# Half of a mixing stage moved into a recurrence, and statistics over two heads at once, in a hand-ordered delta-rule and expert kernel

## The reference

```python
q = short_conv(x @ Wq.T); k = short_conv(x @ Wk.T); v = short_conv(x @ Wv.T)
beta  = sigmoid(x @ Wb.T)
delta = delta_rule(l2norm(q), l2norm(k), v * beta, beta)
short = fir(v, 3 taps per channel); longp = fir(v, 63 taps per channel)
paths = (short, longp, delta, v)
stats = [mean and variance of each path over the 64 of each head]
probs = softmax(gate_mlp(concat(x, stats)) / temp)
probs = maximum(probs, floor); probs /= sum(probs)
out = sum(probs[i] * paths[i])
out = out * rsqrt(mean(out ** 2) + 1e-5) * onorm_w
x1 = layernorm(x + out @ Wo.T)
y  = sum over the top 2 of 8 experts of w * down(silu(gate(x1)) * up(x1))
return layernorm(x1 + y)
```

## Time and profile before

| | |
|---|---|
| median of three runs | 1904.76 us |
| lowest and highest | 1901.11, 1905.17 us |
| the profiled execution's own time | 1897.1 us |
| its span | 1895.4 us |
| mean granted TensorE clock | 0.899 |
| PE busy | 1501.2 us (79%), 12507 instructions |
| PE weight loads (PEld) | 1111.5 us (59%) |
| DVE busy | 1353.1 us (71%), 3875 instructions |
| ACT busy | 949.5 us (50%), 1998 instructions |
| POOL busy | 436.7 us (23%) |
| costliest DVE group: taps of phase B (L1465) | 143.4 us, 192 x 747 ns |

### The profile page before, as it was taken

One profiled execution on the slowest core, in us unless ns is written; L12 is line 12 of the kernel. 1 busy time (PEld: TensorE's weight loads), 2 busy tenths in 40 slices (PEclk: granted clock), 3 DMA queues, 4 the chain that ended last, 5 costly groups with the idle time before them and its releaser, 6 DMA issues. The chain is left out here.

```text
span 1895.4 us, 40891 instructions
## 1 busy us (share of the span) xinstructions
PE 1501.2 (79%) x12507; PEld 1111.5 (59%) x12508; DVE 1353.1 (71%) x3875; ACT 949.5 (50%) x1998; POOL 436.7 (23%) x473
## 2 busy tenths in 40 slices
PE   6776065979999999999999999997436999999800
PEld 3446034737747657657567477476225888888700
DVE  6996055687798887887887887976455455554488
ACT  6772161356455654654655564542443555555434
POOL 6783200000030040040120310300233333333300
PEclk9997586989999999999999999987657999999955
DMA  5548632023243243333342333332524533333295
GB/s 198 191 161 256 168 72 72 3 58 100 73 119 99 60 124 102 79 90 101 93 117 81 93 100 87 93 101 63 190 99 134 188 105 103 101 105 100 79 384 192
DMA packets 297373, 224.36 MB, mean 118 GB/s; under 512 B 173472, under 2 KB 265632, under 8 KB 296960
## 3 DMA queue, kind: packets, MB, share of 16 engines
q1 hardware_dynamic: 225600, 158.84, 28.9%
q0 software_dynamic: 15232, 43.53, 6.3%
q10 hardware_dynamic: 56384, 19.93, 4.1%
HBM read 130.42 MB, written 91.82 MB: 117 GB/s over the span
## 5 line engine op out<-in xcount | busy, mean ns | idle before, releaser
L2041 POOL DMA_INDIRECT y_d<-C_yb,C_dest x136 | 131.6, 968 | 235.0 <-ACT C_yb L2152 232.6
L1465 DVE SCALAR_TENSOR_TENSOR B_conv<-B_ps_x,B_cw,B_conv 128x511 f32<-128x511 f32 (+2 forms) x192 | 143.4, 747 | 51.9 <-ACT B_conv L1177 46.9
L422 POOL DMA_INDIRECT xs_d<-x,slot_u x128 | 133.3, 1042 | 136.7 <-DVE m_acc L1867 100.0
L688 POOL MEMSET B_z<- 128x256 f32 (+4 forms) x40 | 5.6, 199 | 690.7 <-DMA B_z<-scr_a 690.7
L1177 ACT ACTIVATE B_conv<-B_ps_x,B_cw 128x512 f32<-128x512 f32 x64 | 43.7, 683 | 167.2 <-PE B_ps_x L745 165.9
L2271 DVE TENSOR_TENSOR C_av<-C_sg,C_ps_g 128x256 f32<-128x256 f32 x136 | 57.2, 421 | 95.2 <-ACT C_sg L2146 95.2
L745 PE MATMUL B_ps_x<-B_xa,B_wk 128*128 128x512 f32 x128 | 68.1, 660 | 65.8 <-DVE B_sel L1457 45.0
L2075 PE MATMUL C_ps_g<-C_w_high,C_xt_high 128*128 x272 | 120.0, 441 | 0.3 <-DVE C_xt_low L2277 0.3
L2283 DVE TENSOR_TENSOR C_avt_low<-C_ps_a,C_avt_high 128x256 fp32r<-128x256 f32 x136 | 57.6, 424 | 85.2 <-ACT C_avt_high L2141 85.2
L2075 PE MATMUL C_ps_g<-C_w_high,C_xt_low 128*128 x272 | 108.3, 398 | 0.0
L2075 PE MATMUL C_ps_g<-C_w_low,C_xt_high 128*128 x272 | 107.4, 395 | 0.0
(11 more groups left out here) (334 smaller groups left out, 4274.4 us busy)
## 6 DMA issues: line engine op xcount, KB each, us to landing
C_xb<-xs_d SPq DMA_DIRECT2D x136, 132.0 KB, 2.1
C_w_high<-y_d SPq DMA_DIRECT2D x12, 1024.0 KB, 14.0
A_band<-fir_long POOLq DMA_DIRECT2D x32, 256.0 KB, 5.6
A_work<-xT SPq DMA_DIRECT2D x16, 512.0 KB, 4.9
v_d<-A_v_tok SPq DMA_DIRECT2D x16, 512.0 KB, 3.5
short_d<-A_sh_tok SPq DMA_DIRECT2D x16, 512.0 KB, 3.2
B_xa<-xT SPq DMA_DIRECT2D x8, 1024.0 KB, 5.6
B_v_tok<-v_d SPq DMA_DIRECT2D x8, 1024.0 KB, 5.4
```

What stands on the lines that cost most here:

```text
L422: pool.indirect_dma_start(t["xs_d"][:, :], bass.IndirectOffsetOnAxis(ap=slot_u[:, c:c + 1], axis=0), x1[:, b, j, :], None).then_inc(done, 16)
L1465: V.scalar_tensor_tensor(conv[:, g % 2, k:], X[g % 2][:, :SEQ - k], cw[:, g // 4, gg % CH, 3 - k:4 - k], conv[:, g % 2, k:], ALU.mult, ALU ...
L2041: pool.indirect_dma_start(t["y_d"][:, :], bass.IndirectOffsetOnAxis(ap=dest[:, q:q + 1], axis=0), yb[:, u], None).then_inc(y_out[u], 16)
```

## The change

All of it is in phase B.

- **Statistics over two heads.** A `bn_stats` now takes 128 numbers, two heads interleaved (stride 64), so that its even positions are one head and its odd ones the other. There are half as many, and the tile `bn` is half as large. `stats` no longer joins even and odd: five operations in place of nine.
- **Second half batch's mixing.** In merging, DVE still does the softmax, weighs the first half batch's `lo` and `delta` and both half batches' `sh`, and finishes the first half batch. The second half batch's weighing of `lo` and `delta`, its sums, its sum of squares and its scaling (`weigh_long`, `add_delta`, `add_rest`, `sum_squares`, `scale_mix` with b = 1) go to the start of the next step's recurrence. So do its squares and root on ACT (`square_mix`, `rms_root`); its squares go to `hid` in place of `sq`.
- **First key taps.** `taps_of(i + 2, 0)` in merging becomes `taps_of(i + 1, 0)` at the start of recurrence.
- **Output by halves.** PE transposes and projects the first half batch's mix as before, and the second one's in turn 1 of the recurrence, behind `solve_rows` and `within`.
- **Order on DVE in the recurrence and `late_rows`.** Output adds, row statistics and path statistics are placed anew; more statistics are left to `late_rows`.
- **Evictions in one row.** PE makes the four groups of products one after the other, ahead of the router and a projection; DVE and ACT evict the four in a row, and `late_rows` follows DVE's last.
- **Path rows by halves.** SP waits for the transposes of one half batch before it loads that half's rows, where it waited for both.
- **Loop.** DVE's loop is now steps 1 to 6.

```diff
-bnst = sb("bn", [P, PT, PATHS, HEADS, 6]); dm = sb("dm", [P, PT, STATS // 2]); gst = sb("gst", [P, PT, 3, STATS])
+bnst = sb("bn", [P, PT, PATHS, HEADS, 3]); gst = sb("gst", [P, PT, 3, STATS])
...
-squares = sq[:].rearrange("p c (a b) -> p (c a) b", b=D)
+squares = [x.rearrange("p c (a b) -> p (c a) b", b=D) for x in (sq[:], hid[:, 0:2])]
...
-            hold(sp, o_turned, 4 * i)
             for b in range(2):
+                hold(sp, o_turned, 4 * (i - 1) + 2 * (b + 1))
...
-            for jj in range(2):
+            for jj in range(4):
+                if jj > 1:
+                    for k in a_kept:
+                        pe.wait_ge(k, 4 * p + jj - 1)
                 a_products(p, jj)
             if last is not None:
                 router(last)
             project(p, 6)
-            for jj in range(2, 4):
-                for k in a_kept:
-                    pe.wait_ge(k, 4 * p + jj - 1)
-                a_products(p, jj)
             pe.wait_ge(beta_ok, 2 * (p + 1))
...
-                project_out(i - 1, 1)
...
+                if has_prev and s == 1:
+                    turn_mix(i - 1, 1)
...
+                if has_prev and s == 1:
+                    project_out(i - 1, 1)
...
+                if b:
+                    pe.wait_ge(ln, LN * i + m + 1)
...
-            pe.wait_ge(o_kept, 4 * (i + 1))
+            pe.wait_ge(o_kept, 4 * i + 2 * (b + 1))
             for jp in range(2):
-                if b:
-                    pe.wait_ge(ln, LN * i + jp + 1)
...
-                turn_mix(i - 1)
+                turn_mix(i - 1, 0)
...
-                keep_o(i - 1)
+                keep_o(i - 1, 0)
             if has_next:
                 group_b(i + 1, 0)
+            if has_prev:
+                square_mix(i - 1, 1)
+            if has_next:
                 group_a(i + 1, 1)
+            if has_prev:
+                rms_root(i - 1, 1)
             for s in range(1, TPB):
+                if s == 1:
+                    keep_u(i, s)
+                    if has_prev:
+                        keep_o(i - 1, 1)
                 if has_next:
                     group_b(i + 1, s)
                     group_a(i + 1, s + 1)
                 if has_prev and s == 3:
                     keep_x1(i - 1, 0)
-                keep_u(i, s)
+                if s > 1:
+                    keep_u(i, s)
                 if has_prev and s == 2:
...
+            weigh_values(i, 0)
+            if has_next:
+                merge(i + 1, 0)
+            weigh_values(i, 1)
+            if has_next:
+                merge(i + 1, 1)
             if has_after:
                 group_a(i + 2, 0)
+            if has_next:
+                merge(i + 1, 2)
+            square_mix(i, 0)
+            rms_root(i, 0)
             if has_next:
                 merge(i + 1, 3)
                 merge(i + 1, 4)
...
-            for jj in range(2):
+            for jj in range(4):
                 keep_even(jj)
             if not first:
                 late_rows(p - 1)
-            for jj in range(2, 4):
-                keep_even(jj)
...
+                for m in range(CH):
+                    out = bnst[:, n_, (0, 1, 3, 2)[k], 2 * m:2 * m + 2, :].rearrange("p h s -> p (h s)")
+                    w = V.bn_stats(out, src[:, m * P:(m + 1) * P].rearrange("p (h d) -> p d h", h=2))
...
+            if has_next:
+                taps_of(i + 1, 0)
+            if has_prev:
+                weigh_long(i - 1, 1)
+                add_delta(i - 1, 1)
             state(0)
+            if has_prev:
+                add_rest(i - 1, 1)
+            bn(0, 2)
+            bn(1, 2)
             output(0)
             if has_prev:
+                sum_squares(i - 1, 1)
             residual(1)
             if has_prev:
+                scale_mix(i - 1, 1)
+                add_out(i - 1, 0)
+            if has_next:
+                taps_of(i + 1, 1)
             state(1)
+            dve.wait_ge(r_out, 4 * i + 1)
+            bn(0, 3)
             output(1)
             if has_prev:
+                row_stats(i - 1, 0)
+
+            residual(2)
+            if has_next:
+                taps_of(i + 1, 2)
+            if has_prev:
                 add_out(i - 1, 1)
                 row_stats(i - 1, 1)
+            bn(2, 2)
+            bn(3, 2)
+            state(2)
+            output(2)
             if has_next:
                 taps_of(i + 1, 3)
             if has_prev:
                 scale_norm(i - 1)
 
             residual(3)
             dve.wait_ge(r_out, 4 * i + 2)
             bn(1, 3)
+            dve.wait_ge(sl_in[0], 16 * (1 + 2 * HEADS) * (i + 1))
+            for q in range(TPB):
+                bn(q, 0, (0,))
+                if q == 1 and has_next:
+                    taps_of(i + 1, 4)
+            bn(0, 1, (0,))
+            bn(1, 1, (0,))
             output(3)
             if not has_next:
                 late_rows(i)
 
         def late_rows(i):
+            bn(2, 1, (0,))
+            bn(3, 1, (0,))
+            dve.wait_ge(sl_in[1], 16 * (1 + 2 * HEADS) * (i + 1))
+            for q in range(TPB):
+                bn(q, 0, (1,))
+                bn(q, 1, (1,))
+            dve.wait_ge(r_out, 4 * i + 3)
+            bn(2, 3)
             dve.wait_ge(r_out, 4 * i + 4)
             bn(3, 3).then_inc(st_dve, 1)
 
...
+            part = lambda k: gst[:, :, k].rearrange("p t (a s) -> p t a s", s=2)
+            high, low = part(0), part(1)
...
+            V.tensor_copy(high[:, :, :, 0].bitcast(F32R), f[:, :, :, 1]).then_inc(st_dve, 1)
+            V.tensor_scalar(high[:, :, :, 1].bitcast(F32R), f[:, :, :, 2], 1.0 / DH, None,
+                            ALU.mult).then_inc(st_dve, 1)
+            dve.wait_ge(st_dve, c + 3)
+            V.tensor_tensor(low[:, :, :, 0], f[:, :, :, 1], high[:, :, :, 0], ALU.subtract).then_inc(st_dve, 1)
+            V.scalar_tensor_tensor(low[:, :, :, 1], f[:, :, :, 2], 1.0 / DH, high[:, :, :, 1], ALU.mult,
+                                   ALU.subtract).then_inc(st_dve, 1)
...
+        def merge_and_mix(i, has_next):
             softmax(i)
+            weigh_long(i, 0)
+            for b in range(2):
+                weigh_short(i, b)
             if has_next:
                 merge(i + 1, 0)
+            add_delta(i, 0)
+            add_value(i, 0)
+            if has_next:
+                merge(i + 1, 1)
             add_rest(i, 0)
             if has_next:
                 merge(i + 1, 2)
+            add_value(i, 1)
             sum_squares(i, 0)
             if has_next:
                 merge(i + 1, 3)
             scale_mix(i, 0)
             if has_next:
                 first_rows(i + 1)
                 merge(i + 1, 4)
...
-        taps_of(1, 0)
...
-        with dve.Fori(1, PAIRS - 2) as i:
+            merge_and_mix(i, has_next)
+        step(0, False, True)
+        with dve.Fori(1, PAIRS - 1) as i:
+            step(i, True, True)
+        step(PAIRS - 1, True, False)
+        weigh_long(end, 1)
+        add_delta(end, 1)
+        add_rest(end, 1)
+        sum_squares(end, 1)
+        scale_mix(end, 1)
```

152 lines of the change are left out of this document (43 added, 109 removed).

## The result

The changed kernel takes 1935.78 us (median of four runs, 1934.89 to 1949.33), the kernel before 1902.93 (four runs, 1898.98 to 1905.17): ratio 1.0197, interval [1.0165, 1.0229]. (The ratio is not the quotient of the two medians, which is 1.0173; by its interval the change costs 31 to 44 us.) By the medians it is slower, as forecast, but by 33 us where 13 were predicted, and 3.8 us beyond the upper end of the range.

The account below looks back on a forecast made before the run. No engine was taken to bound the kernel throughout; when DVE reaches `scale_norm` decides the A stage's start. Recurrence +8.0, A stage +11.4, clock +1.8, ends -8.0 make +13.2 us: 1918.0 from the median 1904.76, range 1898 to 1932.

Parts of the forecast that it names:

- upper end: High end of the range, 1932 us: half clock every step, later edge count (1.5), tail's gain lost (3.6).
- The back edge: DVE's loop branch, merging to recurrence: idle of 1.79 us carried over, now before work others wait for; DVE resumes at 863.8 or 864.4.
- its two counts: Branch idle counted from the last operation's end (DVE resumes 863.8, scale_norm +1.35 us) or its start (864.4, +1.9).
- the rival in which the edge hides: DVE fetches while waiting for the last merge: 1.8 x 5 us goes, total +2.4, 1907 us; chance 0.16.
- The clock: PE idle before x1_ok in recurrence brings half clock: 0 to 1.6 us per step, 0.3 taken, +1.8 in all.
- a rare rival: PE's clock falls in every step: 1.6 us instead of 0.3, six times, +21, 1926 us; chance 0.08.
- The A stage: Four evictions in a row, then a longer late_rows, delay the query taps: +1.9 us in steps 1 to 6, +11.4.
- Statistics: 128-wide bn_stats at 0.20 us, no stride charge; stats about 1.35 us shorter, giving nothing in a steady step.
- both rivals on their price: bn_stats priced per instruction (0.13 us: 1899.5 us; chance 0.18), or stride costing 0.13 us more each (1961 us; chance 0.06).
- The ends: Step 0 -1.7 us, last step -2.7, tail -3.6 (0 to -6); together -8.0.
- The gain in merging: Taking DVE work out of merging gives back PE's 1.67 us wait for DVE's last copy: 1.7 us and no more.

Follow-up runs that it names:

- e4: The changed kernel with the value path's eight statistics moved right behind the branch, ahead of the key taps: 1937.99 us, ratio 1.0194.
- e1: The changed kernel with DVE's steps 1 to 6 written out, so no branch between them: 1912.36 us, ratio 1.0063.
- e8: The kernel before with DVE's steps 1 to 5 written out, so without its four branches: 1897.00 us, ratio 0.9982.
- e9: The change without DVE's branch, A stage order of before, ACT's turn-2 solution copy earlier, six unread matmuls filling PE's layer-norm wait: 1889.67 us, ratio 0.9933.
- e7: The kernel before with only the two-head statistics and the short stats; order, loop and mixing stay: 1885.20 us, ratio 0.9916.
- e12: The kernel before with two-head statistics, output by halves, mixing and first taps left in merging, DVE unrolled and reordered, ACT's solution copy early: 1881.99 us, ratio 0.9885.
- e13: e12 with the second half's sum of squares moved behind the last merge's copies and its scaling behind the first state: 1860.72 us, ratio 0.9768.
- e5: The changed kernel without DVE's branch and with the order of before in the A stage: 1903.15 us, ratio 1.0006.

## Why the prediction was right in sign and short by 20 us

**The back edge** was the step that failed. The prediction let DVE resume 5.5 to 6.1 us behind the start of the last merge; it does so at 7.3 to 7.6. It carried over the old idle of 1.79 us, which stands behind 1.46 us of other work, to a place where the branch comes straight behind a copy that waits for PE. There it is 3.6 to 3.85 (e4: whatever follows), and neither of its two counts holds. And it charged a late start of DVE with that start alone. In fact PE waits behind it, then works at half clock: in the steps with a branch the two residuals are 13.5 to 15.1 us apart, in step 1 12.3 as forecast. Predicted for the recurrence: 1.6 us in five steps and 0 in step 1. Found: 6.6 and 2.1, together 35 us instead of 8. Counted from the last merge, `scale_norm` was forecast at 41.3 in the five steps (by the earlier of the two counts) and came at 46.0: 2.0 us are lost ahead of the first residual, 2.0 between the two, and 0.7 behind the second, where in two of the five steps the clock falls behind the wait for ACT's copy. e1 shows that 23.4 us of the time are the branch. DVE's work itself was sized well: where the clock stays up, e1 has 12.4 us from the second residual to `scale_norm`, forecast 12.5.

The argument against the rival in which the edge hides, that "the old edge came after a dense stretch, yet cost its full 1.79", was wrong too. The row shows that DVE stood idle, not that anybody waited for it: in e8, without the branch, DVE stands idle nearly as long for PE and ACT. e8 is 4 us faster (its interval is 0.6 to 6.5), and its trace shows 0.5 of them in the six steps.

The Trainium skill (Runtime: NRT & Kernel Launch, section Instruction fetch mechanics) says that a taken branch whose target has not been fetched holds the engine up, and that kernels are better unrolled. e1 agrees, with 23.4 us for five branches. How long the engine stood depended here on what was ahead of the branch, 2.1 us against 3.7.

**The clock** was right in mechanism and too small. Forecast: idle of some 4 us on PE in front of `x1_ok`, 0.3 us per step, and 1.6 per step at a chance of 0.08. Found: a wait of 1.57 to 3.56 us, the half clock in some part of every step, 5.4 us on the way from `scale_norm` to the first product and more ahead of it; e9 gained 10.7 by filling one wait. Treating it as a rare rival was the error: a step with a branch makes PE wait for 1.4 us or more at three places, and in the change's trace the clock falls behind the first in all five, and behind the second or the third in every one.

**The A stage** was right: +1.9 us per step in the trace, 11.4 over six, and the three comparisons give 4.9, 9.2 and 10.0 us.

**Statistics**: eight 128-wide ones take 1.66 us, 0.20 each plus what overlaps, as interpolated, and the stride costs nothing; both rivals on their price are out. That they give little in the steady steps was right as well (2.1 us over six in e7). What they give at the ends was too small, in part for the clock's sake (e7).

**The ends** were forecast at -8.0 and came to -14.4: the last step -7.6 for -2.7, the tail -6.1 for -3.6, step 0 and the start -0.7 for -1.7. In the last step this is in part luck: the clock is at 0.50 for 34.9 us of it before and for 17.2 after, which the sum did not have. The tail's wait of 6.60 us is now 2.06, in front of the second half:

```profile
1412.52 0.68 DVE L1809 TENSOR_TENSOR x<-x,B_ps_turn 128x512 f32<-128x512 f32 x1
...
1417.30 0.69 DVE L1809 TENSOR_TENSOR x<-x,B_ps_turn 128x512 f32<-128x512 f32 x1 [2.06 <-PE B_ps_turn L1062]
```

**The gain in merging**, "1.7 us and no more" per step, counts the wait alone. Before, `scale_norm` follows it: it comes at 39.0 behind a wait of 0.82 at the merge and at 40.0 behind 1.67. But in each of these steps the clock falls behind the wait; where it did not, in steps 2 and 5 of e8 (waits of 1.32 and 1.03), `scale_norm` came at 38.2 and 37.9. Where the recurrence is shorter, as in e12, the steps whose clock falls there are 2.5 to 3.8 us longer than the one whose clock does not, and taking the wait away gave 21 us (e13).

The medians can be taken as a chain from the kernel before to the change, one group of edits after the other: statistics alone -16.0 (e7), output by halves with mixing and taps in the recurrence and no branch +18.0 (e5 against e7), the A stage +9.2 (e1 against e5), the branch +23.4 (the change against e1): +34.6. Such a chain closes by construction (32.9 was measured against other runs of the kernel before), and in another order its parts can differ, as the A stage's do. What is not settled: how the 18.0 divide between DVE's added work and PE's clock (e9 shows 10.7 for one wait), what decides behind which wait the clock falls, and why an idle of the branch of about 2 us stays behind both amounts of work that were tried. A slip of addition changes nothing: the upper end's terms add up to 1931, not 1932.

## What to carry to other kernels

Look for where a hardware loop's branch falls before moving work across it: in the kernel before it took the place of a wait for other engines and cost next to nothing (e8); as the first thing behind a late result it was paid in full, with all that then waits. Price a stall on the matrix engine with the slow clock that can follow it, and fill it or close it; moving a sum of squares and its scaling, which closed one wait of 0.8 to 1.7 us per step, gave 21 us here. And change one thing at a time: the statistics were a gain of 16 us by themselves, which the rest of the same change hid.

## What the runs showed of the hardware

- A taken branch on DVE left it idle 3.4 to 3.9 us where the last instruction ahead had just waited for PE, 1.7 to 2.2 us where 1.5 to 3.6 us of work without late waits stood ahead; the kind of instruction behind it made no difference (e4).
- `bn_stats` over two interleaved heads (128 numbers, stride 64 words) takes 0.20 us, two single heads 0.26. The 0.20 lies on the line through 64 numbers (0.13) and 256 (0.35) read without a stride, so the stride cost nothing here.
- PE was found at 1.2 GHz behind waits of 0.82 us (the kernel before) up to 3.56 us (the change), and at 2.4 GHz behind others of 0.82 (e12) and 1.32 us (e8); which of several waits in a step it was differed from step to step of one execution. e13, whose longest wait of PE in the recurrence is 0.69 us, has a clock of 1.00 through the step.
